# Attention with a fused feed-forward on Trainium2: row maxima transposed by one matmul instead of four, and spread by VectorE instead of copied by ScalarE

## What is computed

```python
xn = layernorm(x)
q, k, v = split(xn @ W_attn + b_attn)            # 16 heads of 64
att = (q @ k.T) / 8 / temperature + slope[h] * (pos_k - pos_q)
att = where(pos_k <= pos_q, att, -inf)
y = softmax(att) @ v
attn = y @ W_proj + b_proj
wg, wu, wd = w_gate / 127, w_up / 127, w_down / 127   # from int32
ffn = (silu(xn @ wg.T) * (xn @ wu.T)) @ wd.T
out = x + attn + ffn
```

## Time and profile before

| | us |
|---|---|
| median of 3 runs | 1230.04 |
| lowest and highest | 1229.83, 1230.42 |
| the profiled execution | 1233.72 |
| its slowest core (core 0), first to last instruction | 1232.2 |
| the other cores' spans | 1224.6 to 1229.4 |
| PE busy on core 0 | 1139.7 (92%) |
| VectorE (DVE) busy | 588.8 (48%) |
| ScalarE (ACT) busy | 528.7 (43%) |
| GpSimd (POOL) busy | 239.5 (19%) |

### The profile page before, as it was taken

One profiled execution on the slowest core, in us unless ns is written; L12 is line 12 of the kernel. 1 busy time (PEld: TensorE's weight loads), 2 busy tenths in 40 slices (PEclk: granted clock), 3 DMA queues, 4 the chain that ended last, 5 costly groups with the idle time before them and its releaser, 6 DMA issues.

```text
span 1232.2 us, 24735 instructions; the slowest of 8 cores (1224.6 to 1232.2 us)
## 1 busy us (share of the span) xinstructions
PE 1139.7 (92%) x7874; PEld 574.5 (47%) x7874; DVE 588.8 (48%) x1194; ACT 528.7 (43%) x963; POOL 239.5 (19%) x292
## 2 busy tenths in 40 slices
PE   2899899999999999999999999999899689999996
PEld 1333345555555555555555555555454234444442
DVE  4442476666666666676566666667661100100000
ACT  0343335665666565565565655556575100000000
POOL 9000112222212222222222112122123300000000
PEclk9999899999999999999999999999999989999998
DMA  8229004322222332132312102122322441424220
GB/s 191 69 87 192 18 28 83 69 62 47 59 58 65 66 66 58 40 69 63 65 36 52 42 23 57 31 52 65 113 53 95 136 163 69 171 98 171 74 69 34
DMA packets 39724, 94.20 MB, mean 76 GB/s; under 512 B 5824, under 2 KB 26433, under 8 KB 38770
## 3 DMA queue, kind: packets, MB, share of 16 engines
q0 software_dynamic: 10352, 44.05, 16.9%
q1 hardware_dynamic: 28768, 48.45, 12.4%
q10 hardware_dynamic: 482, 0.12, 0.0%
HBM read 90.50 MB, written 27.26 MB: 96 GB/s over the span
## 4 chain that ended last, share of the span: by engine, by line
PE 84%; DVE 7%; issue 4%; POOL 2%; DMA 1%; ACT 1%; DVEq 0%; POOLq 0%; ACTq 0%; SPq 0%
PE ps_gu L701 24%; PE ps_dn L866 14%; PE ps_s L790 9%; PE ps_t L771 9%; PE ps_m L682 8%; PE ps_y L806 5%; PE ps_t L733 5%; PE ps_dn L853 4%; DVE cm L544 4%; DMA hb<-h_sc 1%; PE ps_m L819 1%; PE ps_t L775 1%; PE ps_s L793 1%; PE ps_t L737 1%; PE ps_dn L858 1%
## 5 line engine op out<-in xcount | busy, mean ns | idle before, releaser
L544 DVE TENSOR_REDUCE cm<-ps_s 128x1 f32<-128x512 f32 (+3 forms) x640 | 381.4, 608 | 223.9 <-PE ps_s L790 123.4
L650 ACT ACTIVATE pt<-ps_t 128x512 bf16<-128x512 f32 (+1 forms) x576 | 327.6, 576 | 214.3 <-PE ps_t L771 147.4
L701 PE MATMUL ps_gu<-xnT,wubuf 128*128 128x512 bf16 x768 | 264.0, 382 | 2.1 <-DVE hst L472 1.8
L701 PE MATMUL ps_gu<-xnT,wgbuf 128*128 128x512 bf16 x768 | 261.5, 380 | 1.2 <-ACT kst L593 1.2
L790 PE MATMUL ps_s<-kx,qx 67*128 67x512 bf16 (+3 forms) x640 | 219.3, 351 | 29.1 <-DVE cm L544 28.7
L771 PE MATMUL ps_t<-qx,kx 98*128 98x512 bf16 (+3 forms) x640 | 217.1, 349 | 0.6 <-ACT pt L650 0.6
L417 POOL TENSOR_SCALAR th_s<-th_s 128x512 f32<-128x512 f32 x96 | 59.3, 618 | 662.5 <-ACT th_s L601 662.5
L866 PE MATMUL ps_dn<-wdres,hb 128*128 128x512 bf16 x768 | 170.8, 383 | 13.9 <-DMA hb<-h_sc 13.9
L806 PEld LDWEIGHTS ps_y<-Vt,pt 128*128 128x128 bf16 x2176 | 126.5, 97 | 92.5 <-issue 1.3
L806 PE MATMUL ps_y<-Vt,pt 128*128 128x65 bf16 x2176 | 139.8, 193 | 0.0
L582 DVE SCALAR_TENSOR_TENSOR outsb<-ps_dn,xres 128x512 f32<-128x512 f32 x32 | 20.6, 686 | 226.9 <-PE ps_dn L866 226.9
(11 more groups left out here) (76 smaller groups left out, 799.7 us busy)
## 6 DMA issues: line engine op xcount, KB each, us to landing
h_sc<-hst SPq DMA_DIRECT2D x96, 128.0 KB, 1.7
hb<-h_sc SPq DMA_DIRECT2D x4, 3072.0 KB, 13.9
xstage<-xin SPq DMA_DIRECT2D x16, 512.0 KB, 4.7
xres<-xin POOLq DMA_DIRECT2D x16, 512.0 KB, 4.7
out<-outsb POOLq DMA_DIRECT2D x16, 512.0 KB, 3.0
wgbuf<-wg_r POOLq DMA_DIRECT2D x12, 512.0 KB, 6.9
wubuf<-wu_r POOLq DMA_DIRECT2D x12, 512.0 KB, 9.2
wd_sc<-wd_r POOLq DMA_DIRECT2D x12, 512.0 KB, 9.2
```

The lines of the kernel that those rows point to most:

```text
L544: e.tensor_reduce(cm[:, c0:c0 + 1], ps_s[:, s % 2 * 512:s % 2 * 512 + w], AX.X, AluOpType.max, negate=True).then_inc(sem["v_mx"], 1)
L650: e.activation(pt[t % NPT][:, 0:w], ps_t[:, t % 2 * 512:t % 2 * 512 + w], AF.Exp).then_inc(sem["a_e"], 1)
L701: mm = e.matmul(ps_gu[:, r // 8 * 512:r // 8 * 512 + 512], w[:, w0:w0 + 128], xnT[:, dc * T + tb * 512:dc * T + tb * 512 + 512], start=(dc ...
```

## The change

The maxima of a unit (four query tiles, each with a high and a low part: eight columns) now lie side by side in columns 96 to 103 of a narrow `nm`, so that one matmul with the identity puts them on eight partitions of `ps_m`, 128 columns wide. `KT` goes from 98 to 104. Row 96 + 2i + c holds part c of query tile i, for 128 queries. To make of this the 8 x 512 block below q, VectorE multiplies the 128 columns, repeated four times, with a constant 8 x 512 tile `tile_s` that is one where the row belongs to the query tile and zero elsewhere; it writes `qx` directly. ScalarE's copy is gone, with its semaphore `a_m`; `v_m` takes its place. The constant tile is one more load of the start (8 loads in place of 7).

```diff
-KT = 98
+KT = 104
+    tiles = din("tiles", [8, 512], BF16)
+        tile_s = sb(st, "tile_s", [128, 512], BF16)
-        nm = [sb(st, f"nm{i}", [128, 4 * KT], BF16) for i in range(2)]
+        nm = [sb(st, f"nm{i}", [128, KT], BF16) for i in range(2)]
-                    e.memset(kx[q][j][96:98, :], 1.0).then_inc(sem["g_set"], 1)
+                    e.memset(kx[q][j][96:KT, :], 1.0).then_inc(sem["g_set"], 1)
-            e.wait_ge(sem["l_const"], 16 * 7)
+            e.wait_ge(sem["l_const"], 16 * 8)
...
-                        n3 = nm[par].rearrange("p (i c) -> p i c", c=KT)
+                        n3 = nm[par][:, 96:KT].rearrange("p (i c) -> p i c", c=2)
-                        e.tensor_copy(n3[:, :, 96:97], src).then_inc(sem["v_mc"], 1)
+                        e.tensor_copy(n3[:, :, 0:1], src).then_inc(sem["v_mc"], 1)
...
+                if M is not None and M[0] == "m":
+                    n = M[1]
+                    h, b = n // 4, n % 4
+                    e.wait_ge(sem["p_m"], n + 1)
+                    e.tensor_tensor(
+                        qx[h // 2 % 2][h % 2][96:KT, b * 512:(b + 1) * 512].rearrange("p (i q) -> p i q", i=4),
+                        ps_m[96:KT, 0:128].unsqueeze(1).broadcast_to([8, 4, 128]),
+                        tile_s[96:KT, :].rearrange("p (i q) -> p i q", i=4), AluOpType.mult).then_inc(
+                            sem["v_m"], 1)
...
-                if M[0] == "m":
-                    n = M[1]
-                    h, b = n // 4, n % 4
-                    e.wait_ge(sem["p_m"], n + 1)
-                    e.activation(qx[h // 2 % 2][h % 2][96:98, b * 512:(b + 1) * 512], ps_m[96:98, :],
-                                 AF.Copy).then_inc(sem["a_m"], 1)
...
                     if T0[n] == t:
-                        e.wait_ge(sem["a_m"], n + 1)
+                        e.wait_ge(sem["v_m"], n + 1)
...
-                    for i in range(4):
-                        mm = e.matmul(ps_m[0:KT, i * 128:(i + 1) * 128], nm[n % 2][:, i * KT:(i + 1) * KT],
-                                      ident_s[:, :], start=(i == 0), stop=(i == 3))
-                    mm.then_inc(sem["p_m"], 1)
+                    e.matmul(ps_m[0:KT, 0:128], nm[n % 2][:, :], ident_s[:, :], start=True,
+                             stop=True).then_inc(sem["p_m"], 1)
...
+    tiles = np.repeat(np.repeat(np.eye(4, dtype=np.float32), 2, axis=0), 128, axis=1)
```

More of the change, by code:

```diff
@@ L41 @@
     "g_set", "g_th", "g_s",
-    "v_t", "v_bp", "v_cbq", "v_ln", "v_xn", "v_q", "v_mx", "v_mc", "v_rc", "v_y", "v_h", "v_out",
-    "a_c", "a_sd", "a_xe", "a_v", "a_k", "a_m", "a_e", "a_yt", "a_th", "a_g",
+    "v_t", "v_bp", "v_cbq", "v_ln", "v_xn", "v_q", "v_mx", "v_mc", "v_m", "v_rc", "v_y", "v_h", "v_out",
+    "a_c", "a_sd", "a_xe", "a_v", "a_k", "a_e", "a_yt", "a_th", "a_g",
     "p_c", "p_xT", "p_v", "p_qk", "p_s", "p_m", "p_t", "p_av", "p_yt", "p_g", "p_u", "p_d",
@@ L288, in build_program @@
             if M[0] == "m":
-                m_users.append(("a_m", M[1] + 1))
+                m_users.append(("v_m", M[1] + 1))
             elif M[0] == "yt":
@@ L563, in _ @@
                             e.wait_ge(sem["p_m"], n - 1)
-                        e.tensor_copy(n3[:, :, 96:97], src).then_inc(sem["v_mc"], 1)
+                        e.tensor_copy(n3[:, :, 0:1], src).then_inc(sem["v_mc"], 1)
                         e.wait_ge(sem["v_mc"], c + 1)
-                        e.tensor_tensor(n3[:, :, 97:98], src, n3[:, :, 96:97], AluOpType.subtract).then_inc(
+                        e.tensor_tensor(n3[:, :, 1:2], src, n3[:, :, 0:1], AluOpType.subtract).then_inc(
                             sem["v_mc"], 1)
@@ L608, in _ @@
                              (bqk_s[:, :], battn_qk[:, :]), (temp_s[:, :], temp[:, :]),
-                             (bpj_f[:, :], bproj[:, :])):
+                             (bpj_f[:, :], bproj[:, :]), (tile_s[96:KT, :], tiles[:, :])):
                 e.dma_start(out=dst, in_=src).then_inc(sem["l_const"], 16)
-            e.wait_ge(sem["l_const"], 16 * 7)
+            e.wait_ge(sem["l_const"], 16 * 8)
             V3 = Vt.rearrange("p (g d) -> p g d", d=VW)
@@ L655, in _ @@
                     continue
-                if M[0] == "m":
-                    n = M[1]
-                    h, b = n // 4, n % 4
-                    e.wait_ge(sem["p_m"], n + 1)
-                    e.activation(qx[h // 2 % 2][h % 2][96:98, b * 512:(b + 1) * 512], ps_m[96:98, :],
-                                 AF.Copy).then_inc(sem["a_m"], 1)
-                elif M[0] == "yt":
+                if M[0] == "yt":
                     n = M[1]
@@ L890, in _consts @@
         "masks": masks.astype(BF),
+        "tiles": tiles.astype(BF),
         "slopes": np.ascontiguousarray(np.stack(parts, axis=1)),
```

## The result

The changed kernel takes 1225.82 us (median of 9 executions) beside 1231.42 for the kernel before (9): a ratio of 0.9956, 95% interval 0.994 to 0.9972. That is 0.44% or 5.4 us less; the medians lie 5.6 us apart. A later set gave 0.9952 (0.9935 to 0.9969). 1225.2 was forecast, with a gain of 4.8, counted from 1230.04 for the kernel before.

The account below looks back on a forecast made before the run. PE was taken as the bound, with VectorE the one engine that can stop it. Matmuls saved 11.5, less 2.3, 2.8 and 1.6, leaves 4.8 us: 1230.0 - 4.8 = 1225.2 us, range 1221.0 to 1229.0.

Parts of the forecast that it names:

- What bounds it: Middle of attention: PE works 97.64 of 100 us; only VectorE can stop it, with 28.7 us of waits for reductions.
- What PE saves: The nm matmuls in attention: three of four go, 0.18 us at each of 64 places, 11.5 us gained.
- What ScalarE saves: ScalarE's 64 copies, 37.8 us, go; PE waits only 0.6 us for this engine, so nothing counted.
- What VectorE gets: 64 new VectorE operations of 512 elements on 8 partitions, 0.68 us each, 43.5 us in all.
- the cheap operation: Rival on the new VectorE operation: it costs 0.42 us, the saving stays almost whole, 7.5 us, 1222.5; chance 0.10.
- the dear one: Rival on the new VectorE operation: gain turns to loss at 0.92 us, 1231.9 at 1.0; chance 0.11 for slower.
- The load and the start: Start of kernel: an eighth load of 8 KB may delay VectorE half a microsecond, hidden behind GpSimd's memset.
- Places where it doesn't fit: Attention places where the new VectorE work delays PE or its early arrival is wasted: 2.3, 2.8 and 1.6 us lost.
- The six units: Units 23, 35, 47, 50, 59, 62: new operation delays a short reduction PE needs at once; 2.8 us taken.
- the first item: Nearly all units with n % 4 = 3, four more: PE comes early to a reduction not yet done; 2.3 us lost.
- First T's: First T of units 1 and 2 waits for the new VectorE operation: 0.3 and 1.25 us, together 1.6.
- The clock: Rival: PE's clock dips, 1.8 us lost in one; two more on the slowest core give 1228.8; chance 0.12.

Follow-up runs that it names:

- Experiment 3: The changed kernel with the new VectorE operation made twice in a row into the same place; ratio 1.0178, stage 817.1 us.
- experiment 2: The kernel before with its four matmuls, but ScalarE's 2 x 512 copy made by VectorE instead; ratio 1.0013, stage 796.0 us.
- Experiment 1: The kernel before with one of the four nm matmuls, ScalarE's copy kept; ratio 0.9926, stage 787.0 us.
- experiment 4: The kernel before with 16 one-column memsets at the head of VectorE's list and nothing else; ratio 1.0004, stage 794.5 us.
- Experiment 5: The changed kernel with the new VectorE operation at partition 0 instead of 96, writing to scratch; ratio 0.9975, stage 788.45 us with one dip.

## Why the prediction was right, step by step

- **What bounds it: right.** PE is the bound, VectorE stops it at places, totals decide nothing. Experiment 3 is the strongest evidence: 44.6 us of work on a half-idle engine cost 26.8.
- **What PE saves: right, sized 1.3 too high.** 0.18 x 64 took 0.06 for the remaining matmul, the distance inside a run of four. Alone between other matmuls it holds PE 0.07 to 0.08, and the block of four held 0.238: 0.16 x 64 = 10.2.
- **What ScalarE saves: the step that failed.** "I count nothing" rested on 0.6 us in the list of waits of core 0, which is its line for the exponentials and not "the whole run": the same list has 6.0 us for `xnT` and 1.2 for `kst`, in both kernels. It has no wait for the copy, since on core 0 the clock was at 1.2 GHz from 135 to 145 us and PE itself came late. On core 1 the first T of all waits 0.97 for the copy, queued behind the table load and two gate activations:

```profile
139.67 1.28 ACT L601 ACT_TABLE_LOAD   x1 [6.99 <-PE ps_gu L701]
140.53 0.38 PE L819 MATMUL ps_m<-ident_s,nm 128*98 128x128 bf16 x4
...
142.08 0.59 ACT L660 ACTIVATE qx<-ps_m 2x512 bf16<-2x512 f32 x1
...
142.81 0.38 PE L771 MATMUL ps_t<-qx,kx 98*128 98x512 bf16 x1 [0.97 <-ACT qx L660]
```

  From the `m` to this T 2.28 us pass here and 1.62 after. The other T's don't wait for the copy itself but for an exponential that queues behind it. The longest such wait, of unit 53 beside the `m` of unit 54:

```profile
809.83 0.59 ACT L660 ACTIVATE qx<-ps_m 2x512 bf16<-2x512 f32 x1
...
810.44 0.87 ACT L650 ACTIVATE pt<-ps_t 128x256 bf16<-128x256 f32 x2
...
810.97 0.38 PE L771 MATMUL ps_t<-qx,kx 98*128 98x512 bf16 x1 [0.42 <-ACT pt L650]
```

  By starts it is 0.58, and it is gone after. With one of 0.33 and three of 0.14 the relief is 1.8 us, and experiment 2 shows most of it with the matmuls unchanged. Experiment 1 shows that it would have grown.
- **What VectorE gets: right.** 697 ns for 0.68; the cheap operation (424) and the dear one (over 0.92) both fell. The load and the start cost nothing visible: the first `nm` matmul started at 139.2 to 140.9, before at 139.2 to 143.3.
- **Places where it doesn't fit: right, each by name.** Lost arrivals 0.13 to 0.16, at 12 units where 13 were forecast. The six units 0.60, 0.60, 0.60, 0.55, 0.38 and 0.77 are 3.5, of which 0.6 is in the first item: 2.9 against the 2.8 taken. The size is right but the reason for taking it isn't, and that is luck: I took the middle between overlap and none, and the runs say none, for which my count gave 3.5. That 3.5 is not worked out in the prediction; 0.16 more at each of six places makes its 2.1 only 3.1, near the 2.9 measured. Behind the `m`, the short reduction starts 0.81 to 0.85 us later than before at five of the six (core 1 against core 4), the operation with no overlap on either side. At unit 23 it is 0.74, because VectorE stood 0.11 further ahead; there the kernel before had one of the gaps of experiment 4 (L566 at 431.06 came 0.30 behind L564, not 0.10). It was the rule of the Trainium skill (VectorE: DVE Perf Modes, section "Two Vector instructions with no wait between them") that held: an instruction starting in another group of 32 partitions, and the one that comes back, wait for all earlier ones to finish. Experiment 5 agrees: +31 ns at partition 96, -83 and -71 ns at partition 0.
- **First T's: right.** 1.8 for 1.6, the difference being the missing overlap (0.1 at each).
- **Not in the prediction: unit 47, -1.1 us.** A matter of position in VectorE's stream (experiment 4).
- **The clock: right in kind.** A dip costs 1.5 us and not 1.8, and after the change the slowest core has one fewer than before. Since spans of cores differ anyway, I can't say how much of the 5.6 us between the medians this is.

The result is close to the forecast partly by luck. Errors offset: 1.3 too much for the matmuls against 1.8 and 1.1 of gains not counted. And the absolute time, 1225.82 for 1225.2, hides some of what is left: the kernel before has a median of 1231.42 over nine executions, and the forecast counted from 1230.04 over three.

## What to carry to other kernels

An engine's idle share doesn't price new work on it: lay the new instruction into the trace at every place where it runs, and look at what the bounding engine needs next from that engine's queue. Then place it by those few points: moving 6 of 64 instances behind L474 and one reduction gained 2.8 us on top of the change's 5.9, while moving nearly all of them by a step cost 16.8, through the buffer that they empty. When work leaves an engine, read its waits on several cores and at the stage's start too, add up short ones, and look at what queues behind that work as well as at who waits for it.

## What the hardware showed that I had not expected

- **VectorE pairs.** With all operands in the same partitions an instruction starts about 80 ns before the one ahead ends; at partition 96 between ones at 0 it starts 31 ns after, and so does the next. 0.2 us for each excursion, and the excursion itself 697 ns against 672.
- **Small SBUF operations against GpSimd.** A 128 x 4 operation of 0.17 us took 0.97 to 1.17 in the rows above, a difference of two SBUF tiles as well as a cast of one, when it started soon behind GpSimd's 1.15 us product of two SBUF tiles, and ended with it. After the change 88 reductions of PSUM start during such a product on core 3, and none takes over 0.69. Nor is every small operation on SBUF held: the minimum over `cm` (L557) that starts at 143.23, inside a product, takes its usual 0.16. The Trainium skill (SBUF — State Buffer, section "SBUF: two separate sides") describes a port pair that these two engines lock against each other for an instruction's whole length; the rows agree.
- **Gaps in VectorE's stream.** 0.28 to 0.53 us between neighbours that otherwise stand 0.10 or 0.17 apart, about every 128 instructions; no run shows what makes them. Small alone, they decide who comes first, VectorE or GpSimd. Adding 16 instructions at the head of the list moved them, so two versions of a kernel can differ by 1 us at a place where their code is the same.
